# A 3-D depthwise convolution on TensorE: banded matmuls over transposed rows in place of diagonal ones

## The chip, the cores and the metric

The kernel runs on one core of a Trainium2 chip. The metric is the device time of one execution in microseconds (us), the median of several runs. The core's engines run their own instruction streams side by side: PE (TensorE, matmuls), DVE (VectorE), ACT (ScalarE), POOL (GpSimd) and SP (SyncE, which here only issues DMAs). They meet through semaphores; the transfers themselves are done by 16 DMA engines. SBUF is the on-chip memory of 128 partitions, PSUM the accumulators that PE writes.

## The reference, cut to what matters

The program is a chain of layers; the change touches two steps of the first one, the MLP of a Mamba block on 32 images of 96 channels and 32x32 pixels. The 32 images are four volumes of eight frames (`t` is 8), so that each of the two convolutions is a 3x3x3 depthwise one over (frame, row, column), with zero padding on all three axes, in float32:

```python
def dsconv3d(x, dw_w, dw_b, pw_w, pw_b):
    y = jax.lax.conv_general_dilated(x, dw_w, (1, 1, 1), [(1, 1)] * 3,
            dimension_numbers=('NCDHW', 'OIDHW', 'NCDHW'), feature_group_count=x.shape[1])
    y = jax.nn.gelu(y + dw_b[None, :, None, None, None], approximate=False)
    y = jnp.einsum('bcdhw,oc->bodhw', y, pw_w) + pw_b[None, :, None, None, None]
    return y

def mlp(x, t, h, w, p):
    Bv, N, c = x.shape
    xg = jnp.transpose(x, (0, 2, 1)).reshape(Bv, c, t, h, w)
    xg = dsconv3d(xg, p['dw1_w'], p['dw1_b'], p['pw1_w'], p['pw1_b'])   # 96 channels -> 384
    xg = dsconv3d(xg, p['dw2_w'], p['dw2_b'], p['pw2_w'], p['pw2_b'])   # 384 channels -> 96
    return jnp.transpose(xg.reshape(Bv, -1, N), (0, 2, 1))
```

Each output pixel is a sum of 27 products (18 in a volume's first and last frame), then bias and gelu.

## The kernel before

The program is a list of stages that run one after the other; each takes its own SBUF and PSUM tiles (a `Room`) and ends when its last store has landed. The two depthwise stages are `dw1` (from the DRAM tensor `n2` to `g1`, 96 channels) and `dw2` (from `hid` to `g2`, 384 channels). Between them stands `l0_expand`, the pointwise layer, which the change leaves alone. A third caller of `depthwise`, a 2-D stage of the second layer, stays too.

Before, both stages call `depthwise` (L722). Channels lie on partitions (96, or three tiles of 128), a frame's 1024 pixels along the free axis. A volume tile `vol` holds eight frames, loaded in one DMA (L795). There are 4 such volume tiles in `dw1`, 12 in `dw2`. The taps of each frame are dealt out to engines:

- PE takes 9 taps (6 in edge frames) as matmuls with a diagonal 128x128 weight, in two halves of 16 image rows (L826). Each float32 matmul is two passes in the trace.
- ACT multiplies 5 to 7 taps: one opens the accumulator `acc` (L841), the others go to a product buffer `prod` (L848), and POOL adds each of them to `acc` (L895).
- DVE adds the rest, read-modify-write in PE's PSUM tile `pc` (L925), and merges `pc` and `acc` into `sm` (L916). ACT applies bias and gelu in place (L853), SP stores the frame (L802).

The order is the one in which the loops are written: DVE alternates between two frames, ACT closes a frame pair some products later. The buffers `acc`, `sm` and `pc` are four frames deep, `prod` four products.

## Time and profile before

| | us |
|---|---|
| runs (3): lowest, median, highest | 19503.61, 19526.52, 19530.97 |
| profiled execution's span, first to last instruction | 19501.0 |
| stage dw1, from its first DMA issue to that of the next stage | 6021.95 to 6516.09 |
| stage l0_expand | 6516.09 to 6717.23 |
| stage dw2 | 6717.23 to 8090.56 |

The profile is of one execution. Its own time is not given apart from its span; the span is 2.6 us below the lowest of the three runs and 25.5 us below their median. The rows further down use these words: L is the line of the kernel, an arrow points from what is read to what is written, "x704" counts instructions, "busy" is the time in which at least one of them ran, and "ns of one" the mean length of one, which counts overlaps twice. The idle time behind the second bar is what the engine stood still right before them, with the releaser that ended most of it. PEclk is the granted TensorE clock as a share of its full 2.4 GHz. DMA share is the mean busy share of the 16 DMA engines.

### The profile page before, as it was taken

To read this page: it belongs to the slowest core of one execution; us is meant where nothing else is said; L and a number is where in the kernel's file an instruction comes from. 1 tells how busy PE (TensorE), PEld (TensorE's weight loads), DVE (VectorE), ACT (ScalarE), POOL (GpSimd) and SP (SyncE) were. 2 spreads that over 40 slices of the span, in tenths; PEclk is the share of its full clock that TensorE was granted. 3 is DMA by queue.
4 is the path that set the end of the run, shared out by engine and by line. 5 is a ranking of instruction groups with operands and counts; after the bars stand their busy time and mean duration, and the time that the engine had idled before them with its cause. 6 is when DMAs were issued, how large, how long until landed. Compare 5 with 4: busy or idle time off the path is not lost. (4 is left out here: it accounts for less than half of the span.)

```text
span 19501.0 us, 270283 instructions
## 1 busy us (share of the span) xinstructions
PE 17868.3 (92%) x76040; PEld 10298.3 (53%) x76040; DVE 16959.5 (87%) x13130; ACT 15757.6 (81%) x24566; POOL 13555.7 (70%) x6692
## 2 busy tenths in 40 slices
PE   8799997899978899898989999999999999989798
PEld 3455553555533344334556666666666666637374
DVE  4799998899977499658989999999999999969798
ACT  7699995899954555566789999999999999935556
POOL 0199990899945489435589999999999999900101
PEclk9899998999989999999999999999999999999899
DMA  5788886788884412366733333333333333252313
GB/s 180 226 246 236 249 241 209 234 246 244 242 240 127 171 72 82 131 244 228 276 144 118 110 112 120 110 111 117 111 112 120 111 113 116 101 169 56 103 51 99
DMA packets 820728, 3086.61 MB, mean 158 GB/s; under 512 B 100022, under 2 KB 123290, under 8 KB 794780
## 3 DMA queue, kind: packets, MB, share of 16 engines
q1 hardware_dynamic: 805532, 3020.15, 48.3%
q10 hardware_dynamic: 13824, 50.34, 0.7%
q8 instruction: 596, 9.76, 0.2%
q14 instruction: 776, 6.36, 0.1%
HBM read 2264.79 MB, written 805.32 MB: 157 GB/s over the span
## 5 line engine op out<-in xcount | busy, mean ns | idle before, releaser
L1587 DVE TENSOR_TENSOR_SCAN l1s_h<-l1s_da,l1s_pd 128x1024 f32<-128x1024 f32 x3072 | 6782.9, 2268 | 233.2 <-PE l1s_pd L1519 135.2
L1630 ACT ACTIVATE l1s_dm<-l1s_dut,l1s_bt 128x384 f32<-128x384 f32 x7424 | 4051.9, 602 | 69.8 <-PE l1s_pd L1519 69.7
L1613 ACT ACTIVATE l1s_da<-l1s_dl,l1s_a 128x1024 f32<-128x1024 f32 x3072 | 3491.6, 1137 | 31.0 <-DVE l1s_h L1587 30.0
L1519 PE MATMUL l1s_pd<-l1s_id,l1s_dm 128*128 128x128 f32 x22272 | 2967.4, 274 | 39.1 <-DVE l1s_h L1587 36.2
L1519 PEld LDWEIGHTS l1s_pd<-l1s_id,l1s_dm 128*128 128x128 f32 x22272 | 2557.4, 142 | 495.0 <-issue 287.8
L1493 POOL TENSOR_TENSOR l1s_pb<-l1s_h,l1s_cc 128x1024 f32<-128x1024 f32 x1024 | 2518.9, 2460 | 91.9 <-DVE l1s_h L1587 76.2
L1497 POOL TENSOR_TENSOR l1s_pa<-l1s_sm,l1s_cc 128x1024 f32<-128x1024 f32 x1024 | 2434.6, 2378 | 0.0
L1530 PE MATMUL l1s_py<-l1s_pb,l1s_both 128*128 128x512 f32 x4096 | 2156.4, 608 | 192.9 <-POOL l1s_pb L1493 192.9
L1488 POOL TENSOR_TENSOR l1s_sm<-l1s_h 128x1024 f32<-128x1024 f32 x928 | 2204.5, 2376 | 120.8 <-DVE l1s_h L1587 120.7
L895 POOL TENSOR_TENSOR dw_acc<-dw_acc,dw_prod 128x961 f32<-128x961 f32 (+3 forms) x704 | 1573.4, 2282 | 907.8 <-ACT dw_prod L848 900.2
L1530 PE MATMUL l1s_py<-l1s_pa,l1s_id 128*128 128x512 f32 x4096 | 2113.4, 598 | 0.3 <-POOL l1s_pa L1497 0.3
L2453 POOL TENSOR_TENSOR l0sf_pr<-l0sf_h,l0sf_cc 128x1024 f32<-128x1024 f32 x768 | 1818.9, 2390 | 70.8 <-DVE l0sf_h L2535 55.0
L2453 POOL TENSOR_TENSOR l0sb_pr<-l0sb_h,l0sb_cc 128x1024 f32<-128x1024 f32 x768 | 1818.3, 2389 | 68.0 <-DVE l0sb_h L2535 49.2
L826 PE MATMUL dw_pc<-dw_vol,dw_diag 128*128 128x512 f32 (+7 forms) x4224 | 1763.7, 580 | 55.9 <-DMA dw_vol<-n 28.8
L2198 POOL CAST ffn_h<-ffn_z 128x1024 fp8e5<-128x1024 f16 x128 | 181.2, 1417 | 2252.2 <-DVE ffn_z L2218 2234.4
L925 DVE SCALAR_TENSOR_TENSOR dw_pc<-dw_vol,dw_wt,dw_pc 128x961 f32<-128x961 f32 (+5 forms) x1280 | 1484.6, 1234 | 209.0 <-PE dw_pc L826 205.1
L1513 PEld LDWEIGHTS l1s_pd<-l1s_bd,l1s_dut 128*128 128x128 f32 x4608 | 831.3, 191 | 1464.5 <-issue 822.1
L2491 PE MATMUL l0sf_py<-l0sf_pr,l0sf_id 128*128 128x512 f32 x3072 | 1580.7, 597 | 0.0
L2491 PE MATMUL l0sb_py<-l0sb_pr,l0sb_id 128*128 128x512 f32 x3072 | 1579.1, 596 | 0.0
L826 PEld LDWEIGHTS dw_pc<-dw_vol,dw_diag 128*128 128x128 f32 (+1 forms) x4224 | 774.2, 184 | 1046.3 <-issue 1030.0
L2583 ACT ACTIVATE l0sb_dm<-l0sb_dut,l0sb_bt 128x192 f32<-128x192 f32 x3584 | 1314.5, 444 | 9.5 <-DMA l0sb_dl<-l0dlsb 9.5
L2583 ACT ACTIVATE l0sf_dm<-l0sf_dut,l0sf_bt 128x192 f32<-128x192 f32 x3584 | 1313.5, 443 | 9.9 <-DMA l0sf_dl<-l0dlsf 9.9
(305 smaller groups left out, 31821.2 us busy)
## 6 DMA issues: line engine op xcount, KB each, us to landing
l1s_cc<-crows SPq DMA_DIRECT2D x1024, 512.0 KB, 3.7
l0sf_cc<-l0crowsf SPq DMA_DIRECT2D x512, 512.0 KB, 5.7
l0sb_cc<-l0crowsb SPq DMA_DIRECT2D x512, 512.0 KB, 5.5
l0sf_cc<-l0crowsf SPq DMA_DIRECT2D x512, 256.0 KB, 7.5
l0sb_cc<-l0crowsb SPq DMA_DIRECT2D x512, 256.0 KB, 7.1
dls<-l1p_dl SPq DMA_DIRECT2D x192, 512.0 KB, 7.0
duts<-l1p_dut SPq DMA_DIRECT2D x64, 1536.0 KB, 6.0
l1s_dut<-duts SPq DMA_DIRECT2D x64, 1536.0 KB, 7.2
```

What stands on the lines that cost most here:

```text
L826: mm = pe.matmul(pixels(pc[:, f % 4, :])[:, ys, xs], diag[:, v % tiles, diag_taps.index(tap), :], source(v, f, tap, ys, xs), start=(n == 0 ...
L1488: pool.tensor_tensor(sm[:, rnd % 2, :], h[:, rnd * HT % 4, :], h[:, (rnd * HT + 1) % 4, :], ALU.add)\
L1493: pool.tensor_tensor(pb[:, rnd % 2, :], h[:, (rnd * HT + 2) % 4, :], cc[:, rnd % 4, :], ALU.mult)\
L1497: pool.tensor_tensor(pa[:, rnd % 2, :], sm[:, rnd % 2, :], cc[:, rnd % 4, :], ALU.mult)\
L1519: mm = pe.transpose(pd[:, s % 2, blk * 128:blk * 128 + 128], dm[:, rnd % 2, blk, j * 128:j * 128 + 128], idt[:, :])
L1530: mm = pe.matmul(target[:, hs], weights[:, :], row[:, hs], start=(rnd == 0), stop=(rnd == ROUNDS - 1))
L1587: dve.tensor_tensor_scan(h[:, s % 4, :], da[:, j, :], pd[:, s % 2, :], 0.0, ALU.mult, ALU.add)\
L1613: act.activation(da[:, j, :], dl[:, half, j, :], ACT.Exp, scale=a[:, HT * half + j, n:n + 1])\
L1630: ins = act.activation(dm[:, rnd % 2, blk, :], dut[:, half, blk, :], ACT.Identity, scale=bt[:, half, blk, n:n + 1])
L2453: pool.tensor_tensor(pr[:, s % 4, :], h[:, s % 6, :], cc[:, rnd % 4, j, :], ALU.mult).then_inc(prod, 1)
L2491: mm = pe.matmul(py[:, j, HALVES[half]], idt[:, :], pr[:, s % 4, HALVES[half]], start=(n == 0), stop=(n == N - 1))
L2583: ins = act.activation(out, src, ACT.Identity, scale=b)
```

## The change

Both 3-D stages now call a new function, `volume_conv`. It takes channels in blocks of 32 and always all 32 images of a block. A step is three blocks (one step in `dw1`, four in `dw2`), and it is worked off in two units. In each unit:

- One block goes through TensorE. SP loads eight tiles `raw` (L1018), each of 4 frames x 32 channels on 128 partitions. DVE turns each in 32x32 squares into `xin` (L1222), after which a partition is (frame, column) and the free axis is (image row, channel). For each of the 32 channels, PE multiplies by 128x128 weights that hold a band (the column taps of one channel, and the frame taps within a group of four frames), once for each of three row offsets (L1112), and by six 128x32 edge weights for the frames across the border between two groups (L1120). The moving operand is one channel of `xin`, so its elements lie 32 float32 apart, 128 bytes. ACT adds bias, applies gelu and writes into `stg` at the same 128-byte stride (L1136). In the next unit DVE turns `stg` back, tile by tile (L1232), and SP stores the tiles `ot` (L1039).
- Meanwhile half of the frames of the third block (which puts 4 volumes x 32 channels on 128 partitions, loaded frame by frame, L1033) are done by DVE, ACT and POOL alone, PE without: 11 products of ACT and adds of POOL in an inner frame (7 in an edge one), 15 taps (10) on DVE into its own PSUM tile `pd` (L1259, L1262), a merge (L1240), gelu, a store (L1044).

The band weights come from DRAM, 16 pairs of channels per unit (L1025 to L1027), tables of the host side built from the weights alone. Line numbers of the new function are those of the kernel after.

```diff
--- before.py
+++ after.py
@@ -931,6 +931,348 @@
...
+def volume_conv(nc, stage, src, dst, band, edge, bias, taps_w, steps, func):
+
+    T = 8
+    PAIRS, SLOTS = 16, 4
+    PRODS, RAWS, OUTS = 4, 2, 3
+    UNITS = 2 * steps
+    near = (0, -1, 1)
...
+        opened = (depths[1], 0, 0)
+        rest = [tap for tap in on_grid(depths, near, near) if tap not in ((0, 0, 0), opened)]
+        share = 11 if len(depths) == 3 else 7
+        frames_taps.append(([opened] + rest[len(rest) - share:], [(0, 0, 0)] + rest[:len(rest) - share]))
...
+    def block_of(u):
+        return 3 * (u // 2) + u % 2
+
+    def four_frames(of, u, t):
+
+        first = t % SEQS * FRAMES + t // SEQS * 4
+        return of[first:first + 4, 32 * block_of(u):32 * block_of(u) + 32, :]
+
+    def all_volumes(of, i, f):
+        block = 3 * i + 2
+        return of.rearrange("(v f) c n -> f v c n", f=FRAMES)[f, :, 32 * block:32 * block + 32, :]
...
+        xin = r.sb("xin", [128, 2, T, SIDE, 32])
+        stg = r.sb("stg", [128, T, SIDE, 32])
+        raw = r.sb("raw", [128, RAWS, HW]); ot = r.sb("ot", [128, OUTS, HW])
+        wb = r.sb("wb", [128, SLOTS, 2, 3, 128]); we = r.sb("we", [128, SLOTS, 2, 2, 3, 32])
+        vol = r.sb("vol", [128, FRAMES, HW])
+        acc = r.sb("acc", [128, 4, HW]); prod = r.sb("prod", [128, PRODS, HW]); sm = r.sb("sm", [128, 2, HW])
+        wt = r.sb("wt", [128, steps, 28]); bt = r.sb("bt", [128, UNITS, 32])
+        pc = r.ps("pc", [128, 4, 2, 2, SEQS, SIDE]); pd = r.ps("pd", [128, 2, HW])
...
+                def load_raw(q):
+                    if q < T * UNITS:
+                        if q >= RAWS:
+                            sp.wait_ge(turned, nth(q - RAWS))
+                        sp.dma_start(raw[:, q % RAWS, :], four_frames(src, q // T, q % T)).then_inc(s_raw[q % RAWS], 16)
+
+                def load_weights(q):
+                    if q < PAIRS * UNITS:
+                        k = q % SLOTS
+                        if q >= SLOTS:
+                            sp.wait_ge(mm, nth(2 * (q - SLOTS) + 1))
+                        sp.dma_start(wb[:, k, :, :, :], band[q]).then_inc(s_band[k], 16)
+                        sp.dma_start(we[0:32, k, 0, :, :, :], edge[q, 0]).then_inc(s_band[k], 16)
+                        sp.dma_start(we[96:128, k, 1, :, :, :], edge[q, 1]).then_inc(s_band[k], 16)
+
+                def load_frame(i, f):
+                    if i < steps:
+                        if i > 0:
+                            sp.wait_ge(merged, nth((i - 1) * FRAMES + min(f + 1, FRAMES - 1)))
+                        sp.dma_start(vol[:, f, :], all_volumes(src, i, f)).then_inc(s_vol[f], 16)
+
+                def store_tile(u, t):
+                    if u >= 0:
+                        q = T * u + t
+                        sp.wait_ge(back, nth(q))
+                        sp.dma_start(four_frames(dst, u, t), ot[:, q % OUTS, :]).then_inc(s_ot[q % OUTS], 16)
+
+                def store_frame(i, f):
+                    if i >= 0:
+                        sp.wait_ge(done, nth(i * FRAMES + f))
+                        sp.dma_start(all_volumes(dst, i, f), sm[:, f % 2, :]).then_inc(s_sm[f % 2], 16)
...
+                for u in range(UNITS):
+                    i, s = u // 2, u % 2
+                    for j in range(PAIRS):
+                        load_weights(PAIRS * u + j + 3)
+                        if j < 4:
+                            store_tile(u - 1, 2 * j)
+                            store_tile(u - 1, 2 * j + 1)
+                        if j == 4 and s == 0:
+                            load_frame(i, 5) if i else None
+                            load_frame(i, 6) if i else None
+                            load_frame(i, 7) if i else None
+                        if j == 4 and s == 1:
+                            load_frame(i + 1, 1)
+                            load_frame(i + 1, 2)
+                        if j in (4, 6, 8, 9, 11, 13, 14, 15):
+                            load_raw(T * (u + 1) + (4, 6, 8, 9, 11, 13, 14, 15).index(j) + RAWS)
+                        if j == 5:
+                            store_frame(i if s else i - 1, 2 if s else 6)
+                            store_frame(i if s else i - 1, 3 if s else 7)
+                        if j == 10 and s == 0:
+                            load_frame(i + 1, 0)
+                        if j == 10 and s == 1:
+                            load_frame(i + 1, 3)
+                            load_frame(i + 1, 4)
+                        if j == 13:
+                            store_frame(i, 4 * s)
+                            store_frame(i, 4 * s + 1)
...
+                    x = xin[:, u % 2, :, :, :]
+                    pe.wait_ge(turned, nth(T * u + T - 1))
+                    for c in range(32):
+                        q = 32 * u + c
+                        k = q // 2 % SLOTS
+                        if c % 2 == 0:
+                            pe.wait_ge(s_band[k], 48 * (q // (2 * SLOTS) + 1))
+                            pe.wait_ge(evac, nth(q - 7))
+                        sums = pc[:, q // 2 % 4, q % 2, :, :, :]
+
+                        def own(y):
+                            ys = span(y)
+                            return pe.matmul(sums[:, :, :, ys].rearrange("p h v y -> p (h v) y"), wb[:, k, c % 2, y + 1, :],
+                                             x[:, :, ys.start + y:ys.stop + y, c], start=(y == 0), stop=(y == 1))
+
+                        own(0)
+                        for y in near:
+                            ys = span(y)
+                            for h in range(2):
+                                out = slice(96, 128) if h == 0 else slice(0, 32)
+                                pe.matmul(sums[out, h, :, ys], we[:, k, h, c % 2, y + 1, :],
+                                          x[:, SEQS * (1 - h):SEQS * (2 - h), ys.start + y:ys.stop + y, c],
+                                          start=False, stop=False)
+                        own(-1)
+                        ins = own(1)
+                        ins.then_inc(mm, 1)
...
+                def evacuate(u, c):
+                    q = 32 * u + c
+                    if c == 0 and u:
+                        act.wait_ge(back, nth(T * u - 1))
+                    act.wait_ge(mm, nth(q | 1))
+                    act.activation(stg[:, :, :, c].rearrange("p t y -> p (t y)"),
+                                   pc[:, q // 2 % 4, q % 2, :, :, :].rearrange("p h v y -> p (h v y)"), func,
+                                   bias=bt[:, u, c:c + 1]).then_inc(evac, 1)
...
+                def turn_in(u, t):
+                    if u < UNITS:
+                        q = T * u + t
+                        dve.wait_ge(s_raw[q % RAWS], 16 * (q // RAWS) + 16)
+                        if t == 0 and u > 1:
+                            dve.wait_ge(mm, nth(32 * (u - 1) - 1))
+                        dve.transpose(xin[:, u % 2, t, :, :], pixels(raw[:, q % RAWS, :]))\
+                           .then_inc(turned, 1)
+
+                def turn_back(u, t):
+                    if u >= 0:
+                        q = T * u + t
+                        if t == 0:
+                            dve.wait_ge(evac, nth(32 * u + 31))
+                        if q >= OUTS:
+                            dve.wait_ge(s_ot[q % OUTS], 16 * (q // OUTS))
+                        dve.transpose(pixels(ot[:, q % OUTS, :]), stg[:, t, :, :]).then_inc(back, 1)
...
+                        if n == 0 or f == 4 and 4 not in seen:
+                            u, turned_in, start = 2 * i + f // 4, 0, n
+                            for t in range(T):
+                                turn_back(u - 1, t)
...
+                        if (n - start) % 6 == 5 and turned_in < T:
+                            turn_in(u + 1, turned_in)
+                            turned_in += 1
...
@@ -2641,17 +2983,11 @@
     xm, n2, g1 = (dram(n, (IMAGES, C, HW)) for n in ("xm", "n2", "g1"))
     l0_out_proj(nc, x, *ys0, z0, w, xm, n2)
 
-    def frames(i, v):
-        return bass.ds((i * 2 + v) * FRAMES, FRAMES)
-
-    depthwise(nc, "dw1", C, lambda i, v: n2[frames(i, v)].rearrange("b p n -> p b n"),
-              lambda i, v, f: one(g1, (i * 2 + v) * FRAMES + f),
-              w["dw1"], w["dw1_b"], w["ident"][0:C, 0:C], 1, 2, 2, True, ACT.Gelu)
+    volume_conv(nc, "dw1", n2, g1, w["dw1_band"], w["dw1_edge"], w["dw1_bias"], w["dw1_taps"], 1, ACT.Gelu)
     hid, g2 = (dram(n, (IMAGES, 3, 128, HW)) for n in ("hid", "g2"))
     l0_expand(nc, g1, w, hid)
-    depthwise(nc, "dw2", 128, lambda i, v: hid[bass.ds(i * FRAMES, FRAMES), v].rearrange("b p n -> p b n"),
-              lambda i, v, f: one(g2[:, v], i * FRAMES + f),
-              w["dw2"], w["dw2_b"], w["ident"], 3, 3, 4, True, ACT.Gelu)
+    volume_conv(nc, "dw2", hid.rearrange("b t p n -> b (t p) n"), g2.rearrange("b t p n -> b (t p) n"),
+                w["dw2_band"], w["dw2_edge"], w["dw2_bias"], w["dw2_taps"], 4, ACT.Gelu)
...
```

How the streams change can be seen at three places. First SP, which issues all transfers of the two stages. Before, at the start of `dw2`: the loads of three volume tiles, then frame by frame a store.

```order
L795 DMA dw_vol<-hid 128x8x1024 x3
L802 ISA
L802 DMA g<-dw_sm 128x1024
L802 ISA
L802 DMA g<-dw_sm 128x1024
L802 ISA
L802 DMA g<-dw_sm 128x1024
```

After, in `dw1`, near the end of the first unit: a load of `raw`, two stores of the third block's frames (`sm`), then the weights of a pair. `n` is the source in `dw1`, `g` the destination.

```order
L1018 DMA dw_raw<-n 128x1x1024
L1044 DMA g<-dw_sm 4x32x1024 x2
L1025 DMA dw_wb<-in_dw_band 128x768
L1026 DMA dw_we<-in_dw_edge 32x192
L1027 DMA dw_we<-in_dw_edge 32x192
```

And three pairs of weights later, at the start of the second unit, the stores of turned-back tiles among the weights:

```order
L1039 DMA g<-dw_ot 4x32x1024 x2
L1025 DMA dw_wb<-in_dw_band 128x768
L1026 DMA dw_we<-in_dw_edge 32x192
L1027 DMA dw_we<-in_dw_edge 32x192
L1039 DMA g<-dw_ot 4x32x1024 x2
```

One frame's store of 128 rows has become a store of 4 frames by 32 rows, of the same 512 KB, and the load of 4 MB has become eight loads of 512 KB with the same split (L1018, L1033). Second DVE, from the start of `dw1`. Before:

```order
L901 MEMSET dw_acc 96x4096
L905 TENSOR_SCALAR dw_diag<-dw_id,dw_wt 96x96 x9
L906 UNCONDITIONAL_BRANCH
L906 ISA
L922 REGISTER_ALU
L925 SCALAR_TENSOR_TENSOR dw_pc<-dw_vol,dw_wt,dw_pc 96x1024
```

After, from the same place:

```order
L1222 STREAM_TRANSPOSE dw_xin<-dw_raw 128x1024 x8
L1259 TENSOR_SCALAR dw_pd<-dw_vol,dw_wt 128x1024 x2
L1262 SCALAR_TENSOR_TENSOR dw_pd<-dw_vol,dw_wt,dw_pd 128x32x31 x4
L1222 STREAM_TRANSPOSE dw_xin<-dw_raw 128x1024
L1262 SCALAR_TENSOR_TENSOR dw_pd<-dw_vol,dw_wt,dw_pd 128x992 x2
L1262 SCALAR_TENSOR_TENSOR dw_pd<-dw_vol,dw_wt,dw_pd 128x31x31 x4
L1222 STREAM_TRANSPOSE dw_xin<-dw_raw 128x1024
```

The eight tiles of the first unit are turned before DVE's first tap, those of the next unit stand between its taps, one behind every six; from the second unit on, eight turns back (L1232) stand ahead of the taps. Third PE, before: one diagonal matmul per tap and half.

```order
L826 MATMUL dw_pc<-dw_vol,dw_diag 96x512
L826 MATMUL dw_pc<-dw_vol,dw_diag 96x16x31
L826 MATMUL dw_pc<-dw_vol,dw_diag 96x480
L826 MATMUL dw_pc<-dw_vol,dw_diag 96x15x31
```

After, one channel of a block:

```order
L1112 MATMUL dw_pc<-dw_xin,dw_wb 128x256
L1120 MATMUL dw_pc<-dw_xin,dw_we 32x128 x2
L1120 MATMUL dw_pc<-dw_xin,dw_we 32x4x31 x4
L1112 MATMUL dw_pc<-dw_xin,dw_wb 128x8x31 x2
```

Nine matmuls, of which six have 128 columns or slightly fewer and write only 32 partitions, take the place of 12 to 18 with up to 512 columns for a frame.

## Rows read from the trace of the kernel before

**Rows 1.** The page: span, then busy time, share and instructions of each engine.
```profile
span 19501.0 us, 270283 instructions
PE 17868.3 (92%) x76040; PEld 10298.3 (53%) x76040; DVE 16959.5 (87%) x13130; ACT 15757.6 (81%) x24566; POOL 13555.7 (70%) x6692
```

**Rows 2.** Start in us, length, then SP's DMA issues at the stage borders.
```profile
6021.95 0.35 SPq L85 DMA_DIRECT2D dw_wt<-in_dw  x1
...
6516.09 0.32 SPq L85 DMA_DIRECT2D pw_wt<-in_pw  x1
...
6717.23 0.36 SPq L85 DMA_DIRECT2D dw_wt<-in_dw  x1
...
8090.56 0.35 SPq L85 DMA_DIRECT2D l1in_w<-in_pw  x1
```

**Rows 3.** Windows: us, busy of PE, PEld, DVE, ACT, POOL, PEclk, DMA share, GB/s.
```profile
6022.00:6516.00 494.00, 442.26 (x1056) 172.56 (x1056) 411.42 (x362) 255.11 (x241) 393.21 (x176) 0.95 0.20 51
6517.00:6717.00 200.00, 181.42 (x384) 66.69 (x384) 0.00 (x0) 106.97 (x96) 0.00 (x0) 0.97 0.89 315
6717.00:8090.00 1373.00, 1321.43 (x3168) 601.67 (x3168) 1228.05 (x1084) 761.16 (x720) 1180.16 (x528) 0.98 0.19 74
5700.00:6000.00 300.00, 214.97 (x380) 73.23 (x379) 212.84 (x192) 77.39 (x72) 0.00 (x0) 0.81 1.00 276
```

**Rows 4.** Groups of both depthwise stages: count, busy, ns of one, idle before.
```profile
L826 PE MATMUL dw_pc<-dw_vol,dw_diag 128*128 128x512 f32 (+7 forms) x4224 | 1763.7, 580 | 55.9 <-DMA dw_vol<-n 28.8 <-DMA dw_vol<-hid 21.3 <-DVE dw_sm L916 5.8
L895 POOL TENSOR_TENSOR dw_acc<-dw_acc,dw_prod 128x961 f32<-128x961 f32 (+3 forms) x704 | 1573.4, 2282 | 907.8 <-ACT dw_prod L848 900.2 <-POOL dw_acc L895 7.6
L925 DVE SCALAR_TENSOR_TENSOR dw_pc<-dw_vol,dw_wt,dw_pc 128x961 f32<-128x961 f32 (+5 forms) x1280 | 1484.6, 1234 | 209.0 <-PE dw_pc L826 205.1
L848 ACT ACTIVATE dw_prod<-dw_vol,dw_wt 128x961 f32<-128x961 f32 (+3 forms) x704 | 750.0, 1098 | 332.7 <-POOL dw_acc L895 332.6
L916 DVE TENSOR_TENSOR dw_sm<-dw_pc,dw_acc 128x1024 f32<-128x1024 f32 (+1 forms) x128 | 150.2, 1214 | 3.1 <-DVE dw_pc L925 3.1
L841 ACT ACTIVATE dw_acc<-dw_vol,dw_wt 128x992 f32<-128x992 f32 (+1 forms) x128 | 142.9, 1122 | 452.7 <-DVE dw_sm L916 405.8 <-DMA dw_vol<-n 26.6 <-DMA dw_vol<-hid 19.8
L853 ACT ACTIVATE dw_sm<-dw_sm,dw_bt 128x1024 f32<-128x1024 f32 (+1 forms) x128 | 139.5, 1134 | 66.6 <-DVE dw_sm L916 66.6
```

**Rows 5.** DMA at the start of dw2: rate in 40 slices; issues, KB, us to landing.
```profile
GB/s 52 84 83 210 410 394 425 415 440 425 415 415 410 404 410 410 410 410 415 410 404 410 410 404 410 415 410 404 410 415 404 410 415 410 404 410 415 410 404 410
...
dw_vol<-hid SPq DMA_DIRECT2D x3, 4096.0 KB, 23.0
```

**Rows 6.** DMA issues later in dw2, and in stage l0pf.
```profile
g<-dw_sm SPq DMA_DIRECT2D x94, 512.0 KB, 2.8
...
l0crowsf<-l0pf_dts SPq DMA_DIRECT2D x14, 128.0 KB, 2.6
...
l0btsf<-l0pf_bt SPq DMA_DIRECT2D x14, 128.0 KB, 1.7
```

**Rows 7.** Groups of other stages: PE passes of 256 and of 128 columns.
```profile
L1974 PE MATMUL att_px<-att_fe,att_te 128*96 128x256 f32 x1024 | 232.0, 379 | 0.0
...
L1519 PE MATMUL l1s_pd<-l1s_id,l1s_dm 128*128 128x128 f32 x22272 | 2967.4, 274 | 39.1 <-DVE l1s_h L1587 36.2 <-ACT l1s_dm L1630 2.8
```

**Rows 8.** Timeline of PE in l0pf: 512-column passes, 128 and then 64 output columns.
```profile
501.88 1.98 PE L485 MATMUL l0pf_pd<-l0pf_dts,l0pf_wd 128*128 128x512 f32 x4 [1.11 <-ACT l0pf_dts L529]
...
521.23 1.94 PE L488 MATMUL l0pf_pd<-l0pf_dts,l0pf_wd 128*64 128x512 f32 x8 [2.00 <-DVE l0pf_dl L436]
```

**Rows 9.** Group of another stage: ACT reading 256 elements of PSUM.
```profile
L1925 ACT ACTIVATE att_yv<-att_pm,att_col 96x256 f32<-96x256 f32 x64 | 35.5, 554 | 42.5 <-DVE att_xo L2124 29.8 <-PE att_pm L2023 12.7
```

**Rows 10.** DVE: a group of one-input operations.
```profile
L1063 DVE TENSOR_SCALAR l1in_xc<-l1in_xo,l1in_stats 96x1024 f32<-96x1024 f32 x32 | 24.0, 750 | 1.1
```

**Rows 11.** Timeline of POOL and DVE in the second layer, side by side.
```profile
9298.96 2.37 POOL L1251 TENSOR_TENSOR l1p_dl<-l1p_dl,l1p_ln 128x1024 f32<-128x1024 f32 x1 [2.21 <-ACT l1p_ln L1371]
...
9300.23 2.19 DVE L1280 TENSOR_TENSOR l1p_du<-l1p_dl,l1p_u 128x1024 f32<-128x1024 f32 x1
```

More of the change, by code:

```diff
@@ L2739, in arranged, with volume_tables @@
         w[f"skip_{d}"] = pair_tiles(v[f"L0_conv_D_{d}"])
-    w["dw1"] = v["L0_conv_dw1_w"].reshape(C, 1, 27)
-    w["dw1_b"] = column(v["L0_conv_dw1_b"])
+    def volume_tables(taps, offsets):
+        blocks = taps.reshape(-1, 3, 32, 27)
+        steps = len(blocks)
+        cubes = blocks[:, :2].reshape(steps * 2, 32, 3, 3, 3)
+        rows = np.zeros((3, steps * 2, 32, 3, 32, 32), f)
+        for z in range(3):
+            for x in range(3):
+                to = np.arange(max(0, 1 - x), min(32, 33 - x))
+                rows[z][:, :, :, to + x - 1, to] = cubes[:, :, z, :, x, None]
+        rows = rows.transpose(0, 1, 2, 4, 3, 5).reshape(3, steps * 16 * 2, 2, 32, 3, 32).swapaxes(2, 3)
+        band = np.zeros((steps * 32, 4, 32, 2, 3, 4, 32), f)
+        for to in range(4):
+            for of in range(max(0, to - 1), min(4, to + 2)):
+                band[:, of, :, :, :, to] = rows[of - to + 1]
+        flat = blocks[:, 2].repeat(4, axis=0).reshape(steps, 4, 32, 27).reshape(steps, 128, 27)
+        parts = offsets.reshape(steps, 3, 32)
+        last = parts[:, 2].repeat(4, axis=0).reshape(steps, 128, 1)
+        return {"band": band.reshape(steps * 32, 128, 2, 3, 128), "edge": np.stack([rows[2], rows[0]], 1),
+                "bias": np.broadcast_to(parts[:, :2].reshape(1, steps * 2, 32), (128, steps * 2, 32)),
+                "taps": cat([flat, last], 2).swapaxes(0, 1)}
+    for name in ("dw1", "dw2"):
+        for part, table in volume_tables(v[f"L0_conv_{name}_w"], v[f"L0_conv_{name}_b"]).items():
+            w[f"{name}_{part}"] = table
     w["pw1"] = v["L0_conv_pw1_w"].T
     w["pw1_b"] = tiles(v["L0_conv_pw1_b"], 3)
-    w["dw2"] = tiles(v["L0_conv_dw2_w"].reshape(HID, 27), 3)
-    w["dw2_b"] = tiles(v["L0_conv_dw2_b"], 3)
     w["pw2"] = tiles(v["L0_conv_pw2_w"].T, 3)
```

167 lines of the change are left out of this document (added).

## The prediction, made blind

> **What bounds the kernel now.** I read the page's engine shares first. PE is busy 92%, DVE 87%, ACT 81%, POOL 70% of 19501.0 us [rows 1], but that averages some twenty stages, and two of them change. SP's issues at the stage borders give their size [rows 2]: dw1 6516.09 − 6021.95 = 494.1 us, dw2 8090.56 − 6717.23 = 1373.3 us, together 1867.5 us. The windows [rows 3] show what fills dw2: PE 1321 of 1373 us, DVE 1228, POOL 1180, ACT 761, at a clock of 0.98, with the DMA engines at 0.19 only. The groups [rows 4] show who waits: PE stands still 55.9 us in both stages, mostly for the first volume; DVE 209 us, of which 205 for PE's sums. So PE ends last, DVE and POOL are close behind, and transfers are only seen at a stage's start: three loads of 4 MB landed 23.0 us after issue at the median while the engines moved about 410 GB/s [rows 5].
>
> **What the change removes.** All 4224 passes of L826 (1763.7 us busy), 1280 taps, 128 merges, 704 products and adds [rows 4].
>
> **What it adds, by unit.** There are 2 units in dw1 and 8 in dw2. A step needs per inner frame 15 DVE taps and 11 products, per edge frame 10 and 7, so 110 taps and 80 products a step, 55 and 40 a unit.
>
> DVE: a tap cost 1484.6 / 1280 = 1.160 us, a merge 150.2 / 128 = 1.174 [rows 4]. The transpose isn't in the trace. A one-input operation of 1024 elements took 0.750 [rows 10], one with two inputs beside a POOL addition 2.19 [rows 11]; I take the merge's 1.174, the nearest of the same size and type. DVE: 55 × 1.160 + 4 × 1.174 + 16 × 1.174 = 87.3 us.
>
> POOL: 40 × 1573.4 / 704 = 40 × 2.235 = 89.4 us. ACT: 40 × 1.065 + 4 × 1.116 + 4 × 1.090 [rows 4] + 32 evacuations of 256 PSUM elements at 0.554 [rows 9] = 69.2 us. Its write at a stride of 128 bytes isn't in the trace; at double (1.1) ACT has 87 us, still beside POOL.
>
> PE, per channel: 3 own matmuls of 256 columns and 6 edge ones of 128, two passes each. 256 columns cost 232.0 / 1024 = 0.227 us a pass, 128 columns 2967.4 / 22272 = 0.133 [rows 7]. Eight passes that fill only 64 output columns took 1.94 us, four with 128 took 1.98 [rows 8]: narrow passes ran in pairs. The edge matmuls fill 32 output columns and alternate between two places, so they may pair: 6 × 0.227 + 6 × 0.133 = 2.16 us, unpaired 2.96. A unit is 69 or 95 us.
>
> Transfers: a unit has 8 loads of raw, 8 stores of ot, 4 loads of vol and 4 stores of sm, 24 of 524,288 bytes, and 16 pairs of weights of 442,368 bytes. On all 16 engines a pair is 442,368 / 410,000 = 1.08 us [rows 5], with its three issues 1.2. The 24 are new in kind: on the DRAM side their outermost dimension is four frames or four volumes, and 32 channels the next. Every large transfer of the trace has at least 16 there, like the 128 rows of the sm store that landed after 2.8 us, or the 16x2x1024 of l0crowsf after 2.6 us [rows 6]. No row shows what a four does. The bounds: dealt over 16 engines, 1.28 us of engine time; dealt by the four over 4 of them, 131,072 bytes on each at 410 / 16 = 25.6 GB/s [rows 5], 5.12 us. I take the second, because the split of a transfer must go by some outer dimension, and a quarter of the engines is what this one gives. Then the 24 queue up on the same four: 24 × 5.12 + 16 × 1.2 = 142.1, with small gaps 143 us a unit, more than DVE's 87, POOL's 89 and PE's 69 to 95.
>
> The Trainium skill ("DMA: Bandwidth & Descriptors", section "Why a DMA increments its semaphore by 16 and not by 1") says that a transfer uses the largest number of engines up to 16 that divides both sides' slowest dimension, and from SP always the lowest-numbered ones. By it four here, the same four each time. No run here shows it yet; the sum by it is the one above, by all sixteen it is rival A's.
>
> **The sum along a stage.** First unit: DVE turns all eight raw tiles before its first tap, and SP issues three frames among them, 11 transfers or some 61 us before PE starts; up to the unit's end 29 transfers and 19 weight pairs pass: 148.5 + 22.8 = 171.3, and landing 1: 172.5 us. In dw1, without a next step, one transfer less (167.5). Middle units 143, six in dw2. DVE's turning back at a unit's start waits there for ot buffers, of which one comes free every 5.1 us: 32 us instead of 9.4, hidden, since the queue is filled by these very stores. The last unit has no loads for a next one: 32 us turning back, 33 adds left at 2.235 = 74, 5 of waits: 111. The end: 8 stores of ot and 2 of sm at 5.12, landing 2.8 and 4 to the next stage: 58.
>
> dw1: 167.5 + 111 + 58 = 336.5. dw2: 172.5 + 6 × 143 + 111 + 58 = 1199.5. Sum 1536, against 1867.5: −331.5. The span becomes 19501.0 − 331.5 = 19169.5. The span before lies 25.5 us below the median of the runs; with the same offset **19195 us**.
>
> Everything else in the two stages is under the transfers. If that cover goes, DVE and POOL bound a unit at 92: that is rival A. Other stages keep their code and layouts: 0.
>
> Bounds of this case: a quarter at 440 / 16 = 27.5 GB/s (the best slice, [rows 5]) gives 4.77 us, a unit of 133.7, 10.74 such units (1536 / 143) make 1436: 19095. With half a microsecond more for each transfer 5.62, 154, 1654: 19313. Range of this case 19080 to 19330.
>
> **Rivals.**
>
> A, all sixteen engines carry each of the 24. For it: nothing in the trace lands later than its bytes explain [rows 5, 6]; against it: no row has such an outer dimension. Then DVE and POOL bound: 87.3 plus about 4 of waiting for ot at each turn, 92 us a unit; 10 × 92 + 2 × 34 for first loads and last stores = 988, −879: 18622 span, 18650. With edge matmuls unpaired PE bounds, 10 × 95 + 68 = 1018: 18677. Chance 0.14.
>
> B, all sixteen engines, but a strided operand or a shared port makes an engine the bound. If PE reads the operand at half speed, a channel is 6 × 0.43 [rows 8] + 6 × 0.227 = 3.94 us, 320 channels + 76 = 1337: −531, 18996. The trace has no moving operand at such a stride, so nothing speaks for or against. If transposes run beside POOL as L1280 did (2.19 us, [rows 11]), DVE pays 16 × 1.1 = 18 us more a unit: 10 × 110 + 68 = 1168, 18827. Chance of the two 0.09. The Trainium skill ("Advanced Engine Details and Errata", section "SBUF Cachelines") says that accesses which land in another 16-byte line each time pay a penalty; no row here shows one, and at 126 us a unit it stays under the forecast's 143.
>
> C, slower: the quarter of engines runs at the rate that engines have under full load. In the stage before dw1 they were busy 1.00 at 276 GB/s [rows 3], 17.25 GB/s each, so 7.6 us for a transfer, 1.6 for a pair. A unit: 24 × 7.6 + 16 × 1.6 = 208, × 10.74 = 2234: +366, 19893. It decides from a unit of 1867.5 / 10.74 = 173.9 us on, that is from 6.3 us a transfer (20.9 GB/s an engine). Against it: that stage has more traffic on all engines; here 19.7 MB in 143 us, 137 GB/s, half its rate. Chance 0.09. (PE would decide from 5.6 us a channel, 2.6 times its price.)
>
> That the stages don't do what is said, I give nothing apart: streams and counts are fixed in the code.
>
> **How the numbers follow.** Forecast 0.68, A 0.14, B 0.09, C 0.09. The range leaves out most of A and all of C: 18850 to 19420, the upper end by transfers at 6 us (a unit of 163). The runs before spread over 27 us (19503.61 to 19530.97), and 0.2%, 39 us, is about what can be told from no change. Faster by more than that: the forecast, A and B, less a little for their slow ends, 0.89. Within 0.2%: 0.02. Slower: C, 0.09.
>
> **What would show it.** Right: transfers of raw, ot, vol and sm land 6.6 us or more after issue and queue up, a weight pair behind them later than alone; the DMA share is 0.25 to 0.35 while DVE and PE wait for DMA, some 50 us a unit; before the first tap of each stage over 50 us pass. Wrong: these land after 2.8 to 3.9 us and DVE and POOL are busy above 90% (A); PE busy near 100% with 256 columns over 0.4 us a pass, or transposes at 2.2 us (B). PE's passes should read 0.227 and 0.133 at full clock, transposes 1.17, evacuations 0.55. A stage that keeps its time in other places than dw1 and dw2 doesn't enter: if one of them moved, the whole sum would need another look.

## The result, and the profile after

The kernel after took 19357.82 us (median of four runs, 19352.99 to 19362.33), the kernel before 19526.12 in runs beside it. The ratio is 0.9918 with a 95% interval of 0.9904 to 0.9932: faster by 168 us, where 331 were forecast. The time lies in the wide range of the forecast (18850 to 19420), but 28 us above the range given for its own case (19080 to 19330), and the gain is half of the forecast's.

SP's issues at the stage borders of the kernel after (start, length, then as in [rows 2]):

```profile
6048.52 1.34 SPq L1018 DMA_DIRECT2D dw_raw<-n  x2
...
6460.44 0.33 SPq L85 DMA_DIRECT2D pw_wt<-in_pw  x1
...
6660.57 1.27 SPq L1018 DMA_DIRECT2D dw_raw<-hid  x2
...
7947.09 0.36 SPq L85 DMA_DIRECT2D l1in_w<-in_pw  x1
```

dw1 takes 411.9 us in place of 494.1, dw2 1286.5 in place of 1373.3: 169.0 us less, which is the whole difference of the medians. (dw1 starts 26.6 us later than in [rows 2]. That comes from the stage before it, whose code is the same: it took 463.8 us in this trace and 435.8 in that of the kernel before. Over all twelve traces dw1 starts between 6022 and 6058 us. The difference of the two spans, 143.4 us, holds it.)

The page's engine shares, to lay beside [rows 1], move by 1 to 3 points:

```profile
span 19357.6 us, 270014 instructions
...
PE 17487.4 (90%) x77576; PEld 10130.4 (52%) x77576; DVE 16194.9 (84%) x12434; ACT 15400.4 (80%) x24406; POOL 12891.4 (67%) x6390
```

A stage now falls into units, and the first of the eight turns back (L1232) marks a unit's end. Windows of the kernel after (columns as in [rows 3]): dw1 before PE's first matmul, the rest of its first unit, its last unit, the turning back behind it, and a middle unit of dw2.

```profile
6049.00:6112.00 63.00, 0.00 (x0) 0.00 (x0) 9.94 (x9) 10.59 (x10) 9.86 (x6) 0.50 0.32 113
6112.00:6263.00 151.00, 137.43 (x582) 59.99 (x584) 77.68 (x68) 55.22 (x71) 81.41 (x37) 0.94 0.30 100
6263.00:6403.00 140.00, 134.91 (x574) 58.39 (x570) 78.18 (x68) 66.03 (x82) 90.41 (x40) 0.98 0.26 86
6403.00:6435.00 32.00, 0.00 (x0) 0.00 (x0) 9.00 (x8) 1.75 (x2) 0.00 (x0) 0.51 0.24 89
7020.00:7169.00 149.00, 136.36 (x576) 59.69 (x574) 87.06 (x75) 65.28 (x81) 90.64 (x40) 0.94 0.39 133
```

PE is busy 135 of 140 us in the unit in which hardly anything is loaded. That is the row that the forecast did not have. The groups of both stages, in the form of [rows 4]:

```profile
L1210 POOL TENSOR_TENSOR dw_acc<-dw_acc,dw_prod 128x961 f32<-128x961 f32 (+2 forms) x400 | 904.9, 2290 | 667.8 <-ACT dw_prod L1158 665.7
L1112 PE MATMUL dw_pc<-dw_xin,dw_wb 128*128 128x248 f32 (+1 forms) x1920 | 899.7, 614 | 233.1 <-DVE dw_xin L1222 147.1 <-DMA dw_we<-in_dw_edge 43.0 <-ACT dw_stg L1136 42.9
L1262 DVE SCALAR_TENSOR_TENSOR dw_pd<-dw_vol,dw_wt,dw_pd 128x992 f32<-128x992 f32 (+1 forms) x510 | 592.6, 1230 | 1.4
L1120 PE MATMUL dw_pc<-dw_xin,dw_we 128*32 128x124 f32 (+1 forms) x3840 | 509.1, 415 | 0.0
...
L1136 ACT ACTIVATE dw_stg<-dw_pc,dw_bt 128x256 f32<-128x256 f32 x320 | 197.6, 731 | 804.1 <-PE dw_pc L1112 598.5 <-DVE dw_ot L1232 205.5
...
L1222 DVE STREAM_TRANSPOSE dw_xin<-dw_raw 128x1024 f32<-128x1024 f32 x80 | 99.3, 1242 | 639.5 <-DMA dw_raw<-hid 511.5 <-DMA dw_raw<-n 128.0
L1232 DVE STREAM_TRANSPOSE dw_ot<-dw_stg 128x1024 f32<-128x1024 f32 x80 | 97.3, 1236 | 277.4 <-DMA g<-dw_ot 261.2 <-ACT dw_stg L1136 16.3
```

DVE stood still 640 us for raw tiles and 261 for stores. By busy time an own pass (one of L1112) took 899.7 / 1920 = 0.469 us, not 0.227, and an edge pass (L1120) 509.1 / 3840 = 0.133. The two groups overlap at their seams, so that 6 × 0.469 + 12 × 0.133 = 4.41 us a channel counts some time twice: both together kept PE busy for 1363.9 us, 4.26 a channel, 136 us a unit. PE's timeline of dw2 shows it (start, length; a group's length runs on into the next one):

```profile
6728.36 2.88 PE L1112 MATMUL dw_pc<-dw_xin,dw_wb 128*128 128x248 f32 x6
6731.17 1.66 PE L1120 MATMUL dw_pc<-dw_xin,dw_we 128*32 128x128 f32 x12
6732.75 2.79 PE L1112 MATMUL dw_pc<-dw_xin,dw_wb 128*128 128x248 f32 x6
6735.47 1.65 PE L1120 MATMUL dw_pc<-dw_xin,dw_we 128*32 128x128 f32 x12
```

From start to start the first six own passes took 2.81 us, 0.468 each, at a granted clock of 0.50; the next six 2.72 us, 0.453 each, at 1.00. A channel at full clock is 6 × 0.453 + 12 × 0.127 = 4.24 us. Transposes took 1.22 to 1.24 us each by busy time, beside POOL's additions (median length 1.245) as without them (1.245), evacuations with their strided writes 197.6 / 320 = 0.62.

How the transfers ran is plainest where nothing else does, at the end of dw1. DVE's timeline (start, length, then the group):

```profile
6402.83 3.50 DVE L1232 STREAM_TRANSPOSE dw_ot<-dw_stg 128x1024 f32<-128x1024 f32 x3 [0.42 <-ACT dw_stg L1136]
6414.41 1.25 DVE L1232 STREAM_TRANSPOSE dw_ot<-dw_stg 128x1024 f32<-128x1024 f32 x1 [8.08 <-DMA g<-dw_ot]
6419.38 1.25 DVE L1232 STREAM_TRANSPOSE dw_ot<-dw_stg 128x1024 f32<-128x1024 f32 x1 [3.73 <-DMA g<-dw_ot]
6424.36 1.25 DVE L1232 STREAM_TRANSPOSE dw_ot<-dw_stg 128x1024 f32<-128x1024 f32 x1 [3.73 <-DMA g<-dw_ot]
```

A buffer comes free every 4.97 us. The DMA view of the same stretch (busy tenths and rate in 40 slices):

```profile
DMA  0002222221222222222222222222222222222222
GB/s 0 0 15 51 51 72 26 51 67 72 97 113 102 108 102 108 102 102 113 102 108 102 108 102 102 113 102 108 102 108 102 108 108 102 108 102 108 102 113 102
```

A little under a quarter of the engines, and a quarter of the 410 GB/s of [rows 5]. Counted packet by packet, the stretch from 6700 to 7900 us has exactly four packets of SP's queue under way in 60% of its time; nine in ten of the 4 KB packets took 0.159 us. 32 such packets in a row are 5.09 us; the forecast had 5.12.

### The profile page after: what moved, and what is told of

Its sections match the earlier page's. It is cut to its first block and busy times, and to the rows that moved or that the text cites. A ratio compares the mean times of both kernels' runs of the same rounds, so it can differ in the third digit from the quotient of the medians.

```text
span 19357.6 us, 270014 instructions
## 1 busy us (share of the span) xinstructions
PE 17487.4 (90%) x77576; PEld 10130.4 (52%) x77576; DVE 16194.9 (84%) x12434; ACT 15400.4 (80%) x24406; POOL 12891.4 (67%) x6390
## 5 line engine op out<-in xcount | busy, mean ns | idle before, releaser
L1210 POOL TENSOR_TENSOR dw_acc<-dw_acc,dw_prod 128x961 f32<-128x961 f32 (+2 forms) x400 | 904.9, 2290 | 667.8 <-ACT dw_prod L1158 665.7
L2813 PEld LDWEIGHTS l0sf_pd<-l0sf_id,l0sf_dm 128*128 128x128 f32 x6144 | 763.0, 142 | 927.5 <-issue 684.1
L2813 PEld LDWEIGHTS l0sb_pd<-l0sb_id,l0sb_dm 128*128 128x128 f32 x6144 | 763.0, 142 | 924.7 <-issue 683.3
L1112 PE MATMUL dw_pc<-dw_xin,dw_wb 128*128 128x248 f32 (+1 forms) x1920 | 899.7, 614 | 233.1 <-DVE dw_xin L1222 147.1
```

Of the source, the lines that this page charges most:

```text
L2813: mm = pe.transpose(pd[:, half, at:at + 128], dm[:, rnd % 2, blk, COLUMNS[j]:COLUMNS[j] + 128], idt[:, :])
```

## The experiments

Stage sums are dw1 plus dw2 from the profiled execution, from the stage's first issue to the next stage's (before 1867.5, after 1698.4). The middle unit is the mean of six. Each run's ratio is against the kernel before, measured beside it: 19519.7 us for e1 to e4, 19515.1 for e5 to e8, 19505.2 for e9 and e10. Between runs of different groups the stage sums are firmer than the medians.

| run | median us | ratio (95%) | sum | first, middle, last unit, end (dw2) |
|---|---|---|---|---|
| after | 19357.8 | 0.9918 (0.9904 to 0.9932) | 1698.4 | 216.9, 145.0, 139.8, 59.9 |
| e1_spread | 19111.3 | 0.9788 (0.9772 to 0.9804) | 1467.6 | 168.0, 135.6, 135.6, 25.3 |
| e2_contig | 19224.6 | 0.9847 (0.9831 to 0.9864) | 1570.8 | 181.1, 143.8, 114.6, 59.8 |
| e3_spread_contig | 18724.0 | 0.9592 (0.9576 to 0.9608) | 1077.5 | 125.0, 97.5, 97.1, 25.3 |
| e4_dvestride | 18747.0 | 0.9602 (0.9586 to 0.9618) | 1097.6 | 125.9, 100.5, 98.1, 25.0 |
| e5_oneplace | 19468.9 | 0.9978 (0.9968 to 0.9988) | 1827.6 | 203.6, 171.5, 171.5, 25.0 |
| e6_loads_only | 18965.0 | 0.9722 (0.9705 to 0.9738) | 1316.8 | 126.1, 120.0, 114.6, 59.4 |
| e7_halves | 19853.7 | 1.0178 (1.0161 to 1.0195) | 2210.1 | 313.0, 199.0, 139.7, 59.8 |
| e8_interleave | 18721.0 | 0.9598 (0.9582 to 0.9614) | 1078.6 | 125.7, 97.4, 97.1, 24.9 |
| e9_lateevac | 18690.2 | 0.9578 (0.9565 to 0.9591) | 1050.3 | 121.7, 94.9, 94.1, 25.1 |
| e10_actloads | 18711.3 | 0.9596 (0.9583 to 0.9609) | 1067.6 | 132.2, 94.6, 93.5, 25.5 |

**e1_spread.** All 24 transfers of a unit in four pieces of 32 rows; the same for vol, ot and sm (not shown), with the waits raised fourfold.

```diff
-                        sp.dma_start(raw[:, q % RAWS, :], four_frames(src, q // T, q % T)).then_inc(s_raw[q % RAWS], 16)
+                        for h in range(4):
+                            sp.dma_start(raw[32 * h:32 * h + 32, q % RAWS, :],
+                                         four_frames(src, q // T, q % T)[h]).then_inc(s_raw[q % RAWS], 16)
```

> Each of the 24 transfers of a unit (raw, ot, vol, sm) is issued as four transfers of 32 rows, so that its outermost dimension is 32 and no longer 4. Everything else as in the kernel after, whose stages dw1 and dw2 took 411.9 and 1286.5 us, 1698.4 together. Theory: the transfers ran on a quarter of the engines (packets of 4 KB took 159 ns, four at a time), and right under them lies PE with 4.37 us a channel (139.8 us for the last unit, which has hardly any transfers). Then loads and stores land after 3 to 5 us, the start before PE's first matmul shrinks from 64 to 30-40 us, the end from 58 to about 35, but the units stay at 140 us: 10 x 140 + 2 x 70 = 1540, about 160 us less than the kernel after, around 19200 us. Rival: PE was stretched only because it waited for weights behind the slow transfers; then a unit falls to the 95 us of the forecast's PE price or the 92 of DVE and POOL, some 1000 us for both stages, around 18660 us.

246 us less than after, where I expected 160: a unit takes 135.6 and not 140, start and end together some 55 and not 70. PE starts at 30 us and the end is 23 to 25, so the transfers did set both. In a unit of 135.6 us PE never stops. Window of a middle unit, then PE's groups in it:

```profile
6900.00:7030.00 130.00, 130.00 (x550) 55.65 (x546) 82.26 (x71) 62.41 (x76) 87.33 (x39) 1.00 0.51 146
```
```profile
L1117 PE MATMUL dw_pc<-dw_xin,dw_wb 128*128 128x248 f32 x186 | 86.4, 612 | 0.0
L1125 PE MATMUL dw_pc<-dw_xin,dw_we 128*32 128x124 f32 (+1 forms) x364 | 48.3, 414 | 0.0
```

At full clock, with no waits, the passes cost 0.465 and 0.133 us by busy time, 86.4 + 48.3 = 134.7 us in a window of 130.0. Without what is counted twice PE has 135.6 / 32 = 4.24 us a channel. PE's price is its own and not borrowed from late weights; the rival falls.

**e2_contig.** PE's operand contiguous, transfers as in after.

```diff
-                                             x[:, :, ys.start + y:ys.stop + y, c], start=(y == 0), stop=(y == 1))
+                                             xf[:, c, :, ys.start + y:ys.stop + y], start=(y == 0), stop=(y == 1))
```

> PE reads 256 neighbouring elements of xin in place of one channel at a stride of 128 bytes; the output is therefore not the convolution's, all counts and sizes are kept. Transfers as in the kernel after. Theory: the stride doubles the 256-column passes (0.469 us each against 0.227 for the same size in another stage). Then they return to about 0.23, PE has 2.2 to 3.0 us a channel, the first unit of a stage falls from 215 to about 173 us and the last from 140 to 111, while the middle units stay at 143 under the transfers: about 150 us less, around 19210 us. Rival: the passes cost 0.47 because of their weights (a 128x128 load of 0.206 us before each) or because they alternate with narrow ones; then nothing changes, 19357 us.

133 us less than after (150 expected). The last unit is 114.6 (the forecast had 111), the first 181 (172.5), the middle ones 144 (143): with PE out of the way the blind sum of 1536 comes out at 1571. Over both stages an own pass costs 573.9 / 1920 = 0.299 us and an edge pass 298.1 / 3840 = 0.078 by busy time; a part of that ran at the lower clock (granted clock 0.72 and 0.80 in the first and last unit of dw1, in which PE was busy 87 of 180 and 66 of 115 us). PE's timeline has both:

```profile
7204.88 2.88 PE L1112 MATMUL dw_pc<-dw_xin,dw_wb 128*128 128x248 f32 x6
7207.69 1.32 PE L1120 MATMUL dw_pc<-dw_xin,dw_we 128*32 128x128 f32 x12
7208.93 1.54 PE L1112 MATMUL dw_pc<-dw_xin,dw_wb 128*128 128x248 f32 x6
7210.40 0.84 PE L1120 MATMUL dw_pc<-dw_xin,dw_we 128*32 128x128 f32 x12
```

From start to start six contiguous own passes took 2.81 us at a granted clock of 0.50 and 1.47 at 1.00, 0.468 and 0.245 each. So the stride costs a factor of 1.85 at full clock and nothing at half.

**e3_spread_contig.** Both edits.

> Both edits together: transfers of 32 rows, and PE's operand contiguous (output not the convolution's). Theory of two bounds lying on each other: only now DVE and POOL bound, 92 us a unit, 10 x 92 + 2 x 40 to 70 = 1000 to 1060 us for both stages against 1698, around 18680 us (18640 to 18740). If one of the two was no bound, this run equals e1 or e2 within 40 us.

The two edits alone save 231 and 128 us of stage time, together 621. Each alone lays bare the other bound. A unit of 97.5 us is now POOL's 40 additions (90) and DVE's work (87) with small waits. PE, by busy time: 522.5 / 1920 = 0.272 and 279.9 / 3840 = 0.073 us a pass. Together its passes kept it busy for 757.6 us, 2.37 a channel against 4.24 in e1.

**e4_dvestride.** A complete kernel: the stride moves from PE's operand to DVE's result.

```diff
-                        dve.transpose(xin[:, u % 2, t, :, :], pixels(raw[:, q % RAWS, :]))\
+                        dve.transpose(xin[:, u % 2, :, :, :].rearrange("p t y c -> p (t y c)")
+                                      .rearrange("p (c t y) -> p t y c", c=32, t=T)[:, t], pixels(raw[:, q % RAWS, :]))\
```

> A complete kernel: transfers of 32 rows, and xin laid out channel by channel, so that the DVE transpose writes its elements 1024 bytes apart and PE reads 256 in a row. If a strided write costs DVE nothing, as in e3. If it costs the transpose as much again (2.5 in place of 1.25 us), DVE has 87.3 + 8 x 1.25 = 97 us a unit plus 4: about 100 us more than e3 in all, around 18780 us. If it costs four times (5 us), 30 us a unit, 18980 us.

DVE's group in both stages:

```profile
L1227 DVE STREAM_TRANSPOSE dw_xin<-dw_raw 128x1024 f32<-128x1024 f32 x80 | 158.7, 1984 | 260.5 <-DMA dw_raw<-hid 230.2 <-DMA dw_raw<-n 30.2
```

1.98 in place of 1.24 us, 1.6 times as much, which lies between the first two cases expected: 8 × 0.74 = 6 us a unit on DVE, of which 3 show (100.5 against 97.5 in e3), in place of some 60 us of PE's time.

**e5_oneplace.** `out = slice(0, 32)` for both kinds of edge matmul, else e1.

> As e1, but all six edge matmuls of a channel write output partitions 0 to 31, where they alternated between 96 to 127 and 0 to 31 (output not the convolution's). Theory: neighbouring edge passes at two places ran side by side; 0.1325 us a pass is half of the 0.265 that 128 strided columns take alone. Then 12 x 0.265 + 6 x 0.465 = 5.97 us a channel, a unit of 191 instead of 135.6 us, about 550 us more than e1: 19660. Rival: they ran one after the other at 0.13 anyway, and nothing changes: 19111.

PE's timeline of one channel, e5, then e1:

```profile
7001.42 2.71 PE L1125 MATMUL dw_pc<-dw_xin,dw_we 128*32 128x128 f32 x12
```
```profile
7001.94 2.78 PE L1117 MATMUL dw_pc<-dw_xin,dw_wb 128*128 128x248 f32 x6
7004.65 1.63 PE L1125 MATMUL dw_pc<-dw_xin,dw_we 128*32 128x128 f32 x12
```

The twelve edge passes do run side by side at two places: 2.71 us at one, 1.63 at two. But alone one costs 0.226, not the 0.265 I expected, so the unit is 171.5 and not 191. The pairing is shown; without it the kernel takes 358 us more (360 of stage time), not 550.

**e6_loads_only.** e4 with the stores left in one piece.

> As e4, but only the loads (raw, vol) are split into 32 rows; the stores (ot, sm) keep the outermost dimension 4 and so, by the theory, 5.1 us on four engines. The four engines then have 12 x 5.1 + 12 x 1.3 + 16 x 1.5 = 101 us a unit, and at a unit's start DVE gets an ot buffer back only every 5.1 us: 32 us in place of 18. A unit 115 to 118 us against 100, the ends 58 against 24: about 1310 us for both stages against e4's 1098, 18960. If only the loads had mattered, it equals e4, 18747.

18965.0, five us off. A unit takes 120.1 us, 2 to 5 more than expected. The ends are back at 57.6 and 59.4 us: the stores set them.

**e7_halves.** Loads in two pieces of 2 × 32 rows, else the kernel after.

> As the kernel after, but each load of raw and vol is issued as two transfers of 2 x 32 rows: the outermost dimension goes from 4 to 2. Theory (the outermost dimension sets the number of engines, always the lowest ones): two engines for each half, both halves on the same two, 64 packets of 0.159 us each, 10.2 us a load: 12 x 10.2 + 12 x 5.1 + 16 x 1.5 = 208 us a unit, some 530 us more than the kernel after, about 19890. Rival (many rows in one transfer, or many transfers in flight, is what counts): smaller transfers help as in e1 or change nothing, 19110 to 19360.

19853.7, slower than before, and 496 us more than after where 530 were expected: a middle unit takes 199 us and not 208. The DMA view of the start of its dw1:

```profile
DMA  1112282111111111111111111111111111111111
GB/s 52 52 59 67 86 283 80 52 52 52 52 56 51 48 52 52 52 52 52 52 56 52 52 52 52 52 52 52 52 52 52 52 52 52 52 52 52 52 52 52
```

Two pieces in flight together move 52 GB/s, half of the 104 of one piece of 4 × 32: two engines, the same for both. In 53% of the time from 6800 to 7800 us exactly two packets of SP's queue are under way. The number of engines went by the outermost dimension (two here, four in the kernel after, and with 32 all of them: e1 has them 0.98 busy at the start of dw2), and not by rows, bytes or the number of transfers. This excludes the rival.

**e8_interleave.** Complete, e4 with five of the turns back between taps.

```diff
-                            for t in range(T):
+                            for t in range(OUTS):
                                 turn_back(u - 1, t)
...
+                        if OUTS + n - start < T:
+                            turn_back(u - 1, OUTS + n - start)
```

> A complete kernel, e4 with another order on DVE: the first three turns back stand together as before, the other five come one behind each of the unit's first five taps. In e4 DVE waited 8 us a unit for stores of ot while its taps could have run. Theory: DVE (92 us of work) then is busy nearly throughout, a unit falls from 100 to 93-95 us, 50 to 70 us in all, about 18690. Rival: ACT writes stg again only when all eight are turned back, PE then waits for ACT, and the unit stays at 100.

A unit goes from 100.5 to 97.4, half of what I expected, and the sum down by 19 us, a third of the 50 to 70. DVE's waits for ot fall from 48 to 15 us in six units, but POOL's for its products only from 59 to 51, ACT's for the turning back from 86 to 71, and PE's for ACT rise from 61 to 85. Waits of e8 from 6614 to 7219 us (engine, line, what it waited for: us, times, longest):

```profile
ACT dw_stg L1141 <- DVE dw_ot L1237: 71.1, 6, 12.1
...
POOL dw_acc L1215 <- ACT dw_prod L1163: 50.7, 10, 7.5
```

**e9_lateevac.** Complete, e8 with `max(14, ...)` for `max(9, ...)` in ACT's plan, so that it doesn't stand at the first evacuation with POOL's products behind it.

> A complete kernel, e8 with one number changed: ACT takes up a unit's evacuations behind 14 of its other operations, not behind 9. In e8 ACT stood 12 us in each unit before its first evacuation, because stg was not yet turned back, and POOL ran out of products for up to 7.5 us behind it. Theory: POOL then waits less, a unit falls from 97 to about 92 us (its 40 additions are 90), some 45 us in all: about 18675. Rival: PE, which may run only eight channels ahead, ends later for it, DVE waits for the last evacuation, and the unit stays at 97: 18720.

A unit of 94.9 us where 92 were expected, the sum 28 us less (45 expected), the median 31 less (18690.2 against 18721.0, from separate comparisons, with ratios to before whose intervals overlap slightly; the stage times are the firmer evidence). It is the fastest version tried, 0.9578 of before and 668 us under after. The same two waits:

```profile
POOL dw_acc L1215 <- ACT dw_prod L1163: 32.0, 10, 5.7
ACT dw_stg L1141 <- DVE dw_ot L1237: 20.3, 6, 6.1
```

**e10_actloads.** Complete, e9 with the first step's eight frames issued by ACT.

> A complete kernel, e9 with the loads of the first step's eight frames issued by ACT at the stage's start, where SP issued them among the raw tiles. SP then has 32 issues instead of 44 before PE can start: about 6 us less for the issues, and the transfers start on two queues. Theory: PE's first matmul comes at 20-24 us instead of 31, in two stages about 15-20 us less than e9. Rival: the engines carry the same bytes and the raw tiles, two buffers deep, are what waits; no change.

Worse, by 17 us of stage time: PE starts at 44 us, not 31. Issues were not what limited the start. DMA issues in the first 32 us of dw1 (KB, us to landing), e10 and then e9:

```profile
dw_vol<-n ACTq DMA_DIRECT2D x32, 128.0 KB, 10.6
dw_raw<-n SPq DMA_DIRECT2D x23, 128.0 KB, 6.4
```
```profile
dw_raw<-n SPq DMA_DIRECT2D x32, 128.0 KB, 3.2
```

The eight frames, free of waits, are under way together with the raw tiles that PE needs first, and these land after 6.4 us in place of 3.2.

## Why the prediction was wrong, point by point

- **The transfers: right.** Four engines, 5.1 us each; 145.0 us for a middle unit against 143, 58 to 60 us for the end against 58, PE's first matmul at 63.6 us against 61, an ot buffer every 5 us. e7 shows the rule, e1 and e6 what it cost. The Trainium skill's rule ("DMA: Bandwidth & Descriptors", section "Why a DMA increments its semaphore by 16 and not by 1") is borne out with four and with two. e7 also shows that two transfers use the same engines; that these are the lowest-numbered ones no view shows. Rival A is excluded.
- **The step that failed: "everything else in the two stages is under the transfers", with PE at 2.16 to 2.96 us a channel.** It measured 4.24. The term is 6 × 0.227 for the own passes; with the strided operand they cost 0.453 at full clock. In middle units PE's 136 us lie under the transfers' 145. But the first unit needs them behind the 64 before its first matmul (64 + 136 = 200, and in dw1 one wait of 13.5 us for edge weights), and the last one has no transfers to hide them under. There the sum is short: first units 47 and 44 us, last units 29 each, the six middle ones 12 together, ends 2. That is 162 us, all of 1698.4 − 1536.
- **How much of it is the stride.** e2 changes PE's operand alone and takes 128 of the 162 away: 34 and 36 of the first units, 25 of each last one, 7 of the middle ones. The other 35 us are left in e2, 13 and 9 of them in the first units. A pair of weights filled the engines for 1.5 us, not 1.2, by an estimate 16 × 0.3 = 5 us a unit. No run separates the rest; its cause stays open.
- **How the numbers were put together.** Rival B had PE's price nearly right (3.94), but I had tied it to sixteen engines, as an alternative to the forecast. Both held: four engines, and the sign that I had given for B, 256 columns over 0.4 us a pass. I compared its 126 us with the middle unit alone and never carried it through the first and the last one, which are 4 of 10 units. The 3.94 was also in part luck: no row has its 0.43 us ([rows 8] give 1.98 / 4 = 0.495 for 512 columns).
- **The wide range** holds the time by luck. Its upper end stood for transfers at 6 us; they took 5.1, and another term made up the difference.
- **Edge passes: right that they pair** (e5), wrong again by the stride: 12 × 0.127 = 1.52 us a channel against the forecast's 0.80. The 0.133 named among the signs was met by chance: it stood for unpaired contiguous passes, and paired strided ones measured it. At full clock and contiguous a channel in e3 is 6 × 0.244 + 12 × 0.064 = 2.23 us, start to start, so 2.16 was a fair price for an operand that this kernel doesn't have.
- **DVE, POOL, ACT: right within 6%, the evacuations within 12%,** and hidden. Transposes 1.22 to 1.24 (1.174 taken), no contention with POOL as in [rows 11], additions 2.26 (2.235), evacuations 0.62 (0.554).
- **Rival C: excluded**; packets kept 0.159 us.

The gain that rival A priced at 879 us was there to be had. e9 gets 817 us of stage time out of it, once the transfers are spread and PE's operand is contiguous.

## What to carry to other kernels

Look at the outermost dimension of every transfer's DRAM side: "4 frames x 32 channels" uses a quarter of the engines, and splitting such a transfer into pieces of 32 rows is worth its four issues. When two resources are both near the bound, work the sum out unit by unit, ramp and drain included, and ask of each which resource is last there; a price that is hidden in steady state is not hidden at the ends. Put a stride where the engine pays least for it: here DVE paid 0.74 us for 1024 elements, eight times a unit, while PE paid 0.2 us on each of 192 own passes and 0.06 on each of 384 edge passes. When two groups of one engine are added up, check the sum against the window: 134.7 us in a window of 130.0 says that something is counted twice.

## What the runs showed of the hardware

- Float32 moving operand at a 128-byte stride: 0.453 us for a pass of about 256 columns at full clock (e1), 0.245 contiguous (e2). At half clock both take 0.468 (after, e2): the contiguous pass goes with the clock, the strided one hardly does. In the kernel after few passes ran at half clock, so the strided figure there rests on few rows. The Trainium skill ("Advanced Engine Details and Errata", section "SBUF Cachelines") has a penalty for accesses that land in another line each time; the trace agrees that there is one, and gives it this size. That the lines are its cause was not tried.
- Narrow passes at two output places ran side by side also in float32: 12 in 1.63 us (e1) against 2.71 (e5).
- Pieces of 32 rows moved 245 GB/s with the engines busy 0.98 (e1, start of dw2), where the loads of 128 rows moved 410 [rows 5]. In e4 one 4 KB packet in ten took 0.318 us or more, against 0.159 in the kernel after. The cause was not tried; the pieces still land after 3 to 4 us.
- Windows in which PE waits part of the time have a mean granted clock of 0.72 (e2, PE busy 87 of 180 us) to 0.88 (e8, 481 of 605 us), a mixture of the levels of 1.2 and 2.4 GHz; in e1, with PE busy throughout 130 us, it was 1.00.
